# Seven constant matmuls on TensorE around the last cross attention batch's projection, in a one-core decoder layer

## The reference

```
x = x + attention(layernorm(x))                    # 16 heads, segments of 64, delta memory
x = x + cross_attention(layernorm(x), ctx_512)     # 16 heads of 16, 128 keys per batch
x = x + experts(layernorm(x))                      # gate -> 8 logits, top 2 of 8 experts
# the part around the change
logits = einsum('bsd,de->bse', layernorm(x), gate_kernel)
top_k_weights, top_k_indices = top_k(logits, 2)
```

## Time and profile before

| what | value |
|---|---|
| median of three runs (lowest, highest) | 554.32 us (553.88, 556.27) |
| the profiled execution: time, span | 555.12 us, 553.4 us |
| mean granted TensorE clock | 0.957 of full |
| PE matmul, PE weight load, DVE, ACT, POOL busy | 91%, 76%, 62%, 58%, 26% |

### The profile page before, as it was taken

The page is one execution under the profiler, slowest core; times in us unless marked ns, Lnnn a source line. Parts: engine busy times, 40 slices in busy tenths (PEclk is TensorE's granted clock), DMA queues, the critical chain, the costliest instruction groups (busy, mean ns, idle before and its releaser), DMA issues. The chain is left out here.

```text
span 553.4 us, 11854 instructions
## 1 busy us (share of the span) xinstructions
PE 501.3 (91%) x4187; PEld 420.3 (76%) x4196; DVE 342.1 (62%) x746; ACT 321.7 (58%) x762; POOL 145.3 (26%) x144
## 2 busy tenths in 40 slices
PE   8989999999999999999999899995656999999970
PEld 3778888888998888888699777774625888888860
DVE  5266666666745666666566477777463666666654
ACT  4377777778616777777672398885204444544430
POOL 5610000003100000000000148998011555555530
PEclk9999999999999999999999899999558999999995
DMA  9511111111100111110000033443222355444517
GB/s 264 166 57 60 57 57 57 57 49 48 55 4 20 59 57 57 57 57 1 1 0 2 2 113 119 152 131 101 76 86 66 116 169 169 144 156 156 172 66 237
DMA packets 24001, 48.05 MB, mean 87 GB/s; under 512 B 2960, under 2 KB 11168, under 8 KB 23968
## 3 DMA queue, kind: packets, MB, share of 16 engines
q1 hardware_dynamic: 19392, 39.60, 22.9%
q0 software_dynamic: 2240, 6.04, 3.2%
q10 hardware_dynamic: 2336, 1.97, 1.2%
HBM read 42.48 MB, written 5.11 MB: 86 GB/s over the span
## 5 line engine op out<-in xcount | busy, mean ns | idle before, releaser
L709 PE MATMUL psum<-a_xt_hi,a_qk_hi 128*128 128x512 f32 x128 | 54.0, 422 | 0.0
L1417 POOL DMA_INDIRECT picks_dram<-x_wout,e_pick_row x23 | 38.7, 1682 | 53.0 <-DVE x_wout L1584 53.0
L621 DVE COPY a_weights_t<-psum 64x256 f32<-64x256 f32 x32 | 13.7, 428 | 60.7 <-PE psum L826 60.7
L709 PE MATMUL psum<-a_xt_hi,a_qk_lo 128*128 128x512 f32 x128 | 50.1, 392 | 0.0
L709 PE MATMUL psum<-a_xt_lo,a_qk_hi 128*128 128x512 f32 x128 | 50.0, 390 | 0.0
L1010 ACT ACTIVATE x_probs<-psum,x_neg_max 128x128 f32<-128x128 f32 x128 | 45.8, 406 | 6.2 <-DVE x_neg_max L1067 6.2
L1458 ACT ACTIVATE e_inner_hi<-psum 128x512 fp32r<-128x512 f32 x23 | 13.7, 598 | 58.4 <-PE psum L1644 58.4
L958 POOL MEMSET x_v_pad<- 128x1024 f32 x1 | 1.0, 952 | 167.5 <-POOLq L257 167.5
L1635 PE MATMUL psum<-expert_w_hi,e_x_hi 128*128 x92 | 39.0, 424 | 2.2 <-DVE e_x_lo L1562 2.2
L840 PE MATMUL psum<-a_weights_t,a_v 64*128 64x64 f32 x256 | 34.9, 276 | 3.5 <-issue 2.6
L979 POOL TENSOR_TENSOR expert_w_lo<-x_xn_t,expert_w_hi 128x1024 fp32r<-128x1024 f32 x16 | 37.7, 2355 | 1.3
(11 more groups left out here) (236 smaller groups left out, 1489.7 us busy)
## 6 DMA issues: line engine op xcount, KB each, us to landing
x_k_t<-in_expert_wo SPq DMA_DIRECT2D x23, 512.0 KB, 3.5
a_qk_raw<-in_wqk SPq DMA_DIRECT2D x32, 256.0 KB, 2.6
x_xn_t<-in_expert_w SPq DMA_DIRECT2D x16, 512.0 KB, 3.9
a_wv_raw<-in_wv SPq DMA_DIRECT2D x17, 256.0 KB, 2.8
x_sb<-in_x SPq DMA_DIRECT2D x2, 512.0 KB, 5.0
x_k_t<-in_wo SPq DMA_DIRECT2D x1, 1024.0 KB, 10.4
x_v<-in_wo SPq DMA_DIRECT2D x1, 1024.0 KB, 12.9
xn_dram<-xn SPq DMA_DIRECT2D x1, 1024.0 KB, 4.5
```

The costliest lines, as they stand in the source:

```text
L621: dve.tensor_copy(weights_t[SEG:P, :, 0:2, :], t_ps[SEG:P, :, 0:2, :]).then_inc(wt_ready, 1)
L709: last = pe.matmul(out, pick_l(left[a], k), pick_r(right[b], k), start=start and n == 0, stop=n == 3 * KD - 1, skip_group_check=not start)
L1417: pool.indirect_dma_start(out=picks_dram, out_offset=bass.IndirectOffsetOnAxis(ap=pick_row[:, tile:tile + 1], axis=0), in_=y_rows[:, slot, ...
```

## The change

TensorE's program gets a helper that repeats one float32 matmul: the identity as weights, 256 columns of the output weights as data, into the first 256 columns of a PSUM bank. Nobody reads the result. Three of them, into bank 0, go between `transpose_inverse(7)` and `project(7)`; four, into bank 3, go behind `project(7)`, ahead of `transpose_xn(0)`. None has a wait or releases anything. Bank 0 last held scores whose exponentials are done by then, bank 3 likewise, and both are written afresh by later transposes.

```diff
             batches(pe, step)
+            def keep_busy(times, bank):
+
+                for _ in range(times):
+                    pe.matmul(c.bank[bank][:, 0:D], c.ident[:, :], c.wout[:, 0, :], start=True, stop=True)
+
             weigh(B - 1)
             transpose_inverse(B - 1)
+            keep_busy(3, 0)
             project(B - 1)
+            keep_busy(4, 3)
 
             def transpose_xn(i):
```

## The result

Eight runs of the changed kernel took 548.91 to 553.5 us, median 551.26, beside eight of the kernel before, 553.7 to 563.25, median 554.9. The ratio is 0.994, with a 95% interval of 0.9913 to 0.9968: 3.3 us faster (0.006 x 554.9), where 1.8 were forecast. The median forecast was 552.5 us, with a range of 550.0 to 554.6. Timed twice more beside other runs of the kernel before, the change gave 0.9947 (0.9915 to 0.998) and 0.9957 (0.9921 to 0.9994), 2.9 and 2.4 us.

The account below looks back on a forecast made before the run. TensorE at half clock was taken to bound the tail of cross attention from 386.98 us. Direct cost 0, clock gain 1.8, after the phase 0: 554.32 - 1.8 = 552.5 us, range 550.0 to 554.6.

Parts of the forecast that it names:

- The price of a block: On TensorE, one float32 block of 256 columns takes 0.43 us at full clock and 0.85 at half.
- The direct cost, 0: Before the tail, projection 0.09 us and transpose 0 1.05 us late, both hidden by waits for VectorE; path cost 0.
- third rival: Blocks meet a clock already low after the gaps from 376.8 to 380.2 us: 4.3 us late, 558.6; chance 0.06.
- What the clock gives back, and how long it stays: In the tail of cross attention, full clock until a fall at 390.2 us: logits at 394.3, gain 1.8 us.
- first rival: In the tail, the clock stays at full up to the logits: gain 3.9 us, 550.4; chance 0.27.
- the fall behind the 512-column blocks: After the phase, the clock before fell 2.3 us after these blocks ended; used as the shortest delay of a fall.
- After the phase, 0: From the logits on, everything moves ahead with them; a clock fall missed or worse placed, plus or minus 1.7, taken as 0.
- the 1.7 worked out ahead: At the first expert tile, the clock's fall from 417.2 to 420.6 us cost half of 3.4 us, 1.7.
- No difference beyond 0.5%: For the whole kernel, no measurable difference 0.60, faster by over 0.5% 0.34, slower by over 0.5% 0.06.

Follow-up runs that it names:

- narrow: The changed kernel with its fourteen block instructions on 8 columns of data instead of 256; median 554.22 us, ratio 1.0027 to the kernel before.
- three_only: The changed kernel with only the three blocks ahead of the projection; median 551.75 us, ratio 0.9992 to the kernel before.
- four_only: The changed kernel with only the four blocks behind the projection; median 552.45 us, ratio 0.9994 to the kernel before.
- double: The changed kernel with fourteen blocks, six ahead of the projection and eight behind it; median 552.76 us, ratio 1.0011 to the kernel before.
- head_fill: The changed kernel plus three blocks ahead of the last transpose of weights and two ahead of the last weigh; median 552.35 us, ratio 0.9992.
- after_c: The changed kernel unaltered, timed and profiled a third time; median 551.28 us, ratio 0.9957 to the kernel before.
- after: The changed kernel's first profile, of the slowest of its eight runs, 553.5 us.
- again: The changed kernel unaltered, timed again for a second profile; median 550.64 us, ratio 0.9947 to the kernel before.
- before_b: The kernel before, unaltered, run once for a third profile; 555.78 us.
- before_a: The kernel before, unaltered, run once for a second profile; 554.07 us.
- hold: The changed kernel plus one 512-column constant matmul behind the first expert tile's transposes; median 550.66 us, ratio 0.9955 to the kernel before.

## Why the prediction was right, and by how much not

| kernel (profile) | tail, us | logits to end, us | second fall |
|---|---|---|---|
| before, three profiles | 16.05, 13.46, 15.76 | 157.14, 157.08, 156.62 | yes, yes, yes |
| changed, three profiles | 12.69, 12.70, 14.18 | 157.70, 155.74, 155.76 | yes, no, no |
| narrow | 16.17 | 156.23 | no |
| three_only, four_only | 11.80, 11.33 | 156.95, 154.84 | no, no |
| double, head_fill | 15.69, 11.86 | 155.45, 158.21 | no, yes |

*The price of a block.* Forecast 0.43 us at full clock; eight instructions took 1.89 us with the last one's drain, and the four extra blocks of `double` 1.72. Right.

*The direct cost, 0.* Right in the profile in which the clock was up: in `after_c` the projection started at 382.74 us (forecast 382.72), the transposes at 385.33 (385.29) and 386.94 (386.98). Wrong in `after` and `again`, where the first blocks met a half clock, the third rival's condition. There the projection came some 0.8 us behind VectorE's product (385.50 against 384.76; 384.17 against 383.33), and transpose 1 stood behind the blocks, no longer behind VectorE. What decided against that rival is what the prediction held against it: the clock came back within the dense stretch, at 384.7 and 383.5 us, and the rest of the tail ran at full. In `before_b` and `narrow`, without wide blocks, it didn't come back in the tail, in `before_a` only at 388.9 us. I gave it 0.06 as a loss; its condition held in two of three profiles, and both times it ended as a gain.

*What the clock gives back, and how long it stays.* This is the mis-sized term. The forecast took one fall for all executions, at 390.2 us, with a gain of 1.8. One profile of three shows it, at 389.75 us, with a tail of 14.18 us against 16.05: 1.9. In the other two the clock stayed up to the logits, the first rival's case, and the tail was 3.4 us shorter. The kernel before also varies, from 13.46 to 16.05. Over three profiles each the mean tail is 15.09 before and 13.19 after: 1.9 us. That mean agrees with the 1.8 by luck, because two errors cancel: I took neither the better case as common nor the kernel before as partly spared. A small slip in the working changes nothing: the fall behind the 512-column blocks came 2.2 us after them (414.98 to 417.2), not 2.3.

*After the phase, 0.* In all three profiles of before the clock fell again at the first expert tile, in one of three of the changed kernel (415.5 to 418.9 us). The part from the logits to the end averages 157.35 us in the five profiles of the table with that fall and 155.83 in the six without, a difference of 1.5 us, near the 1.7 worked out ahead, though over unlike kernels; the means of before and changed differ by 0.55 us. Together 1.9 + 0.55 = 2.45 us, within the 2.4 to 3.3 that the three timings gave. Whether earlier logits make the second fall rarer, or three profiles each fell that way, isn't shown: `narrow`, with logits as late as before, missed it too, and `hold`, built against it, moved the median by less than the noise.

No difference beyond 0.5% was the likeliest outcome to me, at 0.60; by the first timing the gain is 0.6%, just outside it, by the others 0.5 and 0.4%. The cause is shown by `narrow`, with the clocks of all runs. The timings lie 0.6 to 1.5 us over the forecast of 1.8, and that excess is hardly clear of the noise: the first interval reaches down to 1.8 us (0.0032 x 554.9), the other two lower. An excess would fit executions in which the clock stays up to the logits, two profiles of three, but three profiles can't count their share.

## What to carry to other kernels

Constant matmuls in a wait can pay if short work follows on TensorE that would run at half clock and that nothing else delays. What they cost is their time beyond the wait, 0.43 us here for each float32 block of 256 columns, so fill the waits and not the path: with twice the blocks, or with more in the tail, the gain was no longer to be seen. Test the cause with the same instructions on narrow data before believing it, and look at the clock of every run beside the time. And where the clock is the cause, one profile is one draw: the same program had tails of 13.5 and 16.1 us, so sum over several profiles before a term is trusted.

## What the runs showed of the hardware

- With fourteen instructions of 8 columns the clock fell at 382.4 us and stayed at half to the end of the tail, though TensorE was marked busy without a rest from 382.5 to 396.1 us; with 256 columns it stayed up or came back in the profiles taken. `choose`, with 8 columns as well, kept TensorE busy from 390 to 396 us before and never raised it.
- The same program loses the clock at different places: in the kernel before at 386.5, at 382.1 and 392.3, and at 384.3 us; in the changed one at 380.1, 381.4 or 389.8 us.
- VectorE's four normalised batches took the longer, the more of GpSimd's weight splitting ran beside them: 4.20 us with about 3.4 us of it beside the earlier trace rows, 3.42 with 2.5 (`four_only`), 2.93 with 1.8 (`before_a`), 2.46 with 1.3 (`after`, `again`); with GpSimd done, three took 1.03. Where a low clock delays `weigh`, VectorE starts later and meets less of that work, so part of the delay comes back. No run changes GpSimd's work, so that this is the cause isn't isolated.
